# Cross-attention on one core: scores from fp16 pairs, two heads per step, three score banks and two product banks

## The reference

```python
q, k_t, v_t = heads(x @ W_q), heads(text_ehs @ W_k), heads(text_ehs @ W_v)   # 508 text tokens
probs_t = softmax(einsum('bhsd,bhtd->bhst', q, k_t) * Dh ** -0.5)
text_out = einsum('bhst,bhtd->bhsd', probs_t, v_t)
attn_scores = einsum('bhsd,bhnd->bhsn', q, k_ip) * Dh ** -0.5                 # 4 image tokens
qsem = l2norm(einsum('bhst,bte->bhse', probs_t, text_ehs))
sem = einsum('bhse,bne->bhsn', qsem, l2norm(ip_ehs))
probs_ip = softmax(attn_scores + 0.5 * sem) * spatial_mask
out = (text_out + einsum('bhsn,bhnd->bhsd', probs_ip, v_ip)) @ W_out + b_out + x
```

## Time and profile before

| | us |
|---|---|
| median of 3 runs | 1622.18 (1618.69 to 1624.26) |
| profiled execution | 1616.23 |
| span of its trace, first to last instruction | 1614.3 |
| TensorE busy | 1559.7 (97%) |
| VectorE busy | 1306.1 (81%) |
| GpSimd busy | 1257.5 (78%) |
| ACT busy | 1053.4 (65%) |
| mean granted TensorE clock | 0.989 of full speed |

### The profile page before, as it was taken

One profiled execution on the slowest core, in us unless ns is written; L12 is line 12 of the kernel. 1 busy time (PEld: TensorE's weight loads), 2 busy tenths in 40 slices (PEclk: granted clock), 3 DMA queues, 4 the chain that ended last, 5 costly groups with the idle time before them and its releaser, 6 DMA issues.

```text
span 1614.3 us, 39295 instructions
## 1 busy us (share of the span) xinstructions
PE 1559.7 (97%) x13322; PEld 951.1 (59%) x13322; DVE 1306.1 (81%) x3181; ACT 1053.4 (65%) x2289; POOL 1257.5 (78%) x1187
## 2 busy tenths in 40 slices
PE   4999999999999999999999999999999999999996
PEld 2777667556555556555555555555555555555553
DVE  6455563688999978997899789978997899789976
ACT  4455656667776767776777667766776677667761
POOL 4233233789899988997899789988998899889982
PEclk9899999899999999999999999999999999999998
DMA  5455757778789978898889889987898798878963
GB/s 206 132 165 146 202 174 192 151 131 139 134 137 191 154 148 155 164 149 149 153 169 143 148 144 173 147 150 145 171 155 148 147 170 151 148 140 146 160 121 94
DMA packets 656043, 247.89 MB, mean 154 GB/s; under 512 B 619081, under 2 KB 645330, under 8 KB 655858
## 3 DMA queue, kind: packets, MB, share of 16 engines
q1 hardware_dynamic: 654658, 243.75, 78.4%
q10 hardware_dynamic: 1200, 1.80, 0.3%
HBM read 68.51 MB, written 34.55 MB: 64 GB/s over the span
## 4 chain that ended last, share of the span: by engine, by line
PE 78%; DVE 9%; issue 4%; POOL 3%; ACT 3%; DMA 3%; SPq 0%; DVEq 0%; ACTq 0%; POOLq 0%
PE bank L1636 27%; PE bank L1637 17%; PE bank L1689 13%; PE bank L1593 7%; PE bank L1641 3%; PE bank L1603 3%; PE bank L1635 3%; DVE probs L1250 2%; DVE neg_max L1238 2%; DMA late<-wkv 2%; PE bank L1666 2%; PE bank L1750 2%; ACT probs L864 1%; POOL wkv L745 1%; PE bank L1676 1%
## 5 line engine op out<-in xcount | busy, mean ns | idle before, releaser
L1636 PE MATMUL bank<-u_sb,late 127*128 127x508 f16 x2560 | 944.9, 375 | 0.0
L1637 PE MATMUL bank<-u_sb,late 127*128 127x508 f16 (+3 forms) x2560 | 762.1, 298 | 0.0
L1238 DVE TENSOR_REDUCE neg_max<-bank 128x1 f32<-128x508 f32 x640 | 434.7, 679 | 157.4 <-PE bank L1593 156.6
L1635 PE MATMUL bank<-v_ring,late 127*128 127x42 f16 x2560 | 468.2, 183 | 6.9 <-DMA late<-wkv 6.9
L1250 DVE SCALAR_TENSOR_TENSOR probs<-bank,probs 128x508 f32<-128x508 f32 x640 | 431.8, 675 | 5.8 <-PE bank L1637 5.8
L745 POOL TENSOR_TENSOR wkv<-probs,wkv 128x508 f16<-128x508 f32 x320 | 364.8, 1145 | 87.3 <-ACT wkv L876 86.5
L1635 PEld LDWEIGHTS bank<-v_ring,late 127*128 127x128 f16 x2560 | 246.7, 96 | 237.4 <-DMA late<-wkv 8.9
L1636 PEld LDWEIGHTS bank<-u_sb,late 127*128 127x128 f16 x2560 | 247.8, 97 | 185.9 <-issue 1.2
L853 ACT ACTIVATE exp_bias<-neg_max 128x1 f32<-128x1 f32 x512 | 103.8, 203 | 378.5 <-DVE neg_max L1238 376.4
L864 ACT ACTIVATE probs<-bank,exp_bias 128x508 f32<-128x508 f32 x512 | 340.4, 665 | 0.1
L752 POOL TENSOR_TENSOR probs<-probs,wkv 128x508 f32<-128x508 f32 x256 | 290.0, 1143 | 0.0
(11 more groups left out here) (194 smaller groups left out, 1870.6 us busy)
## 6 DMA issues: line engine op xcount, KB each, us to landing
raw<-k_parts SPq DMA_DIRECT2D x192, 79.4 KB, 3.6
raw<-in_ctx_cols SPq DMA_DIRECT2D x8, 1016.0 KB, 7.5
raw<-q_parts SPq DMA_DIRECT2D x32, 240.0 KB, 3.7
...
```

The source lines that it names most:

```text
L1238: nc.vector.tensor_reduce(neg_max[:, v % 4:v % 4 + 1], bank[s_bank(v)][:, 0:T], AX.X, ALU.max, negate=True)\
L1635: nc.tensor.matmul(o, hi_k, v_ring[0:TP, n, h, k, :], start=(k == 0), stop=False)
L1636: nc.tensor.matmul(y, hi_k, u_sb[0:TP, par, GH[k]:GH[k] + T], start=(k == 0), stop=False)
L1637: done = nc.tensor.matmul(y[:, k * TP:T], hi_k, u_sb[0:TP, par, UL[k]:UL[k] + U_COLS[k]], start=False, stop=(k == TT - 1))
```

## The change

- **Scores from fp16 pairs.** Queries and keys are kept as two fp16 parts, unscaled but for a power of two. Their four products are 64 rows. The scale of the scores (`score_unit`) is applied in `shift` and `exp`. All units, plain ones too, get the shift. ACT's casts of the middle part and GpSimd's subtractions in the first phase are gone. Each query part is stored twice.
- **Two heads side by side.** A pair of units, v and v+1, is now heads h and h+10 on the same 128 rows. The score of the first takes rows 0 to 63 of the array, the other one rows 64 to 127. Groups that are loaded together have 4 heads where they had 5.
- **Order.** In every even step TensorE computes both scores of a pair, VectorE both maxima, and ACT shift and exponential of the one and the other, before the rest of either unit.
- **Banks.** Three score banks, two product banks. The products of unit u now need the norm of u-2, and the next pair of scores needs the exponential of the pair's first unit.
- **12 slots of probabilities;** the two more lie in memory that the shorter rings of keys and queries set free.

```diff
-    PAIRS = [(0, 0), (1, 0), (2, 0), (0, 1), (1, 1), (0, 2)]
-    KS = len(PAIRS) * D
+    KS = 4 * D
...
-    PROB_RING, TURN_RING, FLAT_RING, HALF_RING = 10, 7, 8, 4
+    PROB_RING, TURN_RING, FLAT_RING, HALF_RING = 12, 7, 8, 4
...
-    q_parts = nc.dram_tensor("q_parts", [B, 3, D, H, S], bf16).ap()
-    k_parts = nc.dram_tensor("k_parts", [B, 3, D, H, T], bf16).ap()
+    q_parts = nc.dram_tensor("q_parts", [B, 4, D, H, S], fp16).ap()
+    k_parts = nc.dram_tensor("k_parts", [B, 2, D, H, T], fp16).ap()
...
-        parts = late[:, :].bitcast(bf16).rearrange("p (t a s) -> p t a s", t=2 * NC, a=3)
+        parts = late[:, 0:2 * NC * S].bitcast(fp16).rearrange("p (t a s) -> p t a s", t=2 * NC, a=2)
...
-        S_BANKS, PT_BANKS, Y_BANKS, O_BANK = (0, 1), (2,), (3, 4, 5), 6
+        S_BANKS, PT_BANKS, Y_BANKS, O_BANK = (0, 1, 2), (3,), (4, 5), 6
...
+        def place(v):
+
+            pair, rest = divmod(v % OF_BATCH, 2 * ST)
+            return pair + rest % 2 * FAR, rest // 2
...
+        def load_keys(eng, b, i, n):
+
+            for half in range(2):
+                heads = slice(half * FAR + i * GROUP // 2, half * FAR + (i + 1) * GROUP // 2)
+                for copy in range(2):
+                    at = half * KS + copy * 2 * D
+                    eng.dma_start(k_ring[at:at + 2 * D, n], k_parts[b, :, :, heads, :].rearrange("a d h t -> (a d) h t"))\
+                       .then_inc(group_loaded[n], 16)
+
+        def load_queries(eng, b, i, n):
...
-                    dst = (q_parts if t < NC else k_parts)[b].rearrange("a d h s -> (d h) a s")[c0:c0 + cn]
-                    n = S if t < NC else T
-                    sp.dma_start(dst, parts[0:cn, t, :, 0:n]).then_inc(parts_saved, 16)
+                    job = (Q_JOB + K_JOB)[t]
+                    sp.wait_ge(bank_drained[job[0]], use(job, b))
+                    if t < NC:
+                        dst = q_parts[b].rearrange("(a r) d h s -> r (d h) a s", r=2)
+                        for copy in range(2):
+                            sp.dma_start(dst[copy, c0:c0 + cn], parts[0:cn, t, :, 0:S]).then_inc(parts_saved, 16)
+                    else:
+                        dst = k_parts[b].rearrange("a d h s -> (d h) a s")
+                        sp.dma_start(dst[c0:c0 + cn], parts[0:cn, t, :, 0:T]).then_inc(parts_saved, 16)
...
+                if i == 2 and 1 <= g < GROUPS - 1:
+                    next_group(g + 1, load_keys)
+                if i == 5 and 1 <= g < GROUPS - 1:
+                    next_group(g + 1, load_queries)
                 if i == 9 and 1 <= g < GROUPS - 1:
-                    next_group(g + 1)
+                    next_values(g + 1)
...
             def batch(b, first, last):
-
-                for t in range(2 * NC):
-                    cn = CT[t % NC][1]
-                    n = S if t < NC else T
-                    pool.wait_ge(mid_split, 2 * NC * b + t + 1)
-                    nc.gpsimd.tensor_tensor(parts[0:cn, t, 2, 0:n], resid[0:cn, t % R1, 0:n], parts[0:cn, t, 1, 0:n],
-                                            ALU.subtract).then_inc(parts_split, 1)
 
...
             def shift(v):
 
+                b = v // OF_BATCH
                 act.wait_ge(row_max_found, v + 1)
-                nc.scalar.activation(exp_bias[:, v % 4:v % 4 + 1], neg_max[:, v % 4:v % 4 + 1], ACT.Copy, bias=LOG_SCALE)\
-                  .then_inc(bias_ready, 1)
+                nc.scalar.activation(exp_bias[:, v % 4:v % 4 + 1], neg_max[:, v % 4:v % 4 + 1], ACT.Identity, bias=log_col[:, 0:1],
+                                     scale=score_unit[:, b:b + 1]).then_inc(bias_ready, 1)
 
             def exp(v):
 
-                if is_turned(v):
-                    act.wait_ge(bias_ready, nth(v) + 1)
-                else:
-                    act.wait_ge(row_max_found, v + 1)
+                b = v // OF_BATCH
+                act.wait_ge(bias_ready, v + 1)
                 need(act, norms_done, v + 1 - PROB_RING)
-                bias = exp_bias if is_turned(v) else neg_max
-                nc.scalar.activation(probs[:, v % PROB_RING, :], bank[s_bank(v)][:, 0:T], ACT.Exp,
-                                     bias=bias[:, v % 4:v % 4 + 1]).then_inc(probs_ready, 1)
+                if PROB_SLOTS <= v < PROB_RING:
+                    act.wait_ge(in_lo_split, 2 * B)
+                nc.scalar.activation(prob(v), bank[s_bank(v)][:, 0:T], ACT.Exp, bias=exp_bias[:, v % 4:v % 4 + 1],
+                                     scale=score_unit[:, b:b + 1]).then_inc(probs_ready, 1)
 
             def flat_hi(v):
...
 
                 b, j = batch_of(v)
-                if v < TT and is_turned(v):
+                if v < TT:
                     shift(v)
+                    exp(v)
+                elif v < UNITS and v % 2 == 0:
+                    shift(v)
+                    exp(v)
+                    shift(v + 1)
+                    exp(v + 1)
                 if v >= HI_AT and not is_turned(v - HI_AT):
                     hi(v - HI_AT)
-                if v < UNITS:
-                    exp(v)
-                if TT <= v + 1 < UNITS and is_turned(v + 1):
-                    shift(v + 1)
...
-
-
...
                 for t in range(2 * NC):
                     j, c0, cn = (Q_JOB + K_JOB)[t], *CT[t % NC]
                     act.wait_ge(bank_filled[j[0]], use(j, b))
                     if t < NC:
                         nc.scalar.activation(q_full[0:cn, t, :], bank[j[0]][0:cn, 0:S], ACT.Identity,
                                              scale=scale[0:cn, par, Q_COL:Q_COL + 1]).then_inc(q_full_ready, 1)
-                        nc.scalar.activation(parts[0:cn, t, 0, 0:S], bank[j[0]][0:cn, 0:S], ACT.Identity,
-                                             scale=scale[0:cn, par, Q_COL:Q_COL + 1]).then_inc(hi_split, 1)
+                        nc.scalar.activation(parts[0:cn, t, 0, 0:S], bank[j[0]][0:cn, 0:S], ACT.Copy, scale=HEAD_DOWN).then_inc(hi_split, 1)
                     else:
-                        nc.scalar.activation(parts[0:cn, t, 0, 0:T], bank[j[0]][0:cn, 0:T], ACT.Identity,
-                                             scale=scale[0:cn, par, K_COL:K_COL + 1]).then_inc(hi_split, 1)
-                    if t > 0:
-                        middle(t - 1)
+                        nc.scalar.activation(parts[0:cn, t, 0, 0:T], bank[j[0]][0:cn, 0:T], ACT.Copy, scale=HEAD_DOWN).then_inc(hi_split, 1)
...
@@ -1440,8 +1463,11 @@
             def unit(v):
 
                 b, j = batch_of(v)
-                if v < UNITS:
+                if v < TT:
                     row_maximum(v)
+                elif v < UNITS and v % 2 == 0:
+                    row_maximum(v)
+                    row_maximum(v + 1)
                 u = v - NORM_AT
...
-                    n, col = (S, Q_COL) if t < NC else (T, K_COL)
+                    n = S if t < NC else T
                     dve.wait_ge(hi_split, 2 * NC * b + t + 1)
-                    dve.wait_ge(parts_split, 2 * NC * b + t + 1)
-                    nc.vector.scalar_tensor_tensor(resid[0:cn, t % R1, 0:n], bank[j[0]][0:cn, 0:n], scale[0:cn, par, col:col + 1],
+                    nc.vector.scalar_tensor_tensor(parts[0:cn, t, 1, 0:n], bank[j[0]][0:cn, 0:n], HEAD_DOWN,
                                                    parts[0:cn, t, 0, 0:n], ALU.mult, ALU.subtract)\
...
                 for t in range(NC):
                     residual(t)
                 if not last:
...
             def scores(v):
 
-                g, h, st = v // OF_GROUP, v // ST % GROUP, v % ST
-                n = g % 2
+                g, st, half, pr = v // OF_GROUP, place(v)[1], v % 2, v // (2 * ST) % 2
+                n, rows = g % 2, slice(half * KS, (half + 1) * KS)
                 if v % OF_GROUP == 0:
-                    pe.wait_ge(group_loaded[n], 16 * 9 * (g // 2 + 1))
+                    pe.wait_ge(group_loaded[n], 16 * 6 * (g // 2 + 1))
                 if v < len(S_BANKS):
                     pe.wait_ge(bank_drained[s_bank(v)], end_of_phase1(s_bank(v)))
-                need(pe, probs_ready, v + 1 - len(S_BANKS))
-                nc.tensor.matmul(bank[s_bank(v)][:, 0:T], q_ring[:, n, h, st * P:(st + 1) * P], k_ring[:, n, h, :],
+                need(pe, probs_ready, v - v % 2 + 2 - len(S_BANKS))
+                nc.tensor.matmul(bank[s_bank(v)][:, 0:T], q_ring[rows, n, pr, st * P:(st + 1) * P], k_ring[rows, n, pr, :],
...
-                if v + LEAD < UNITS:
+                y, o = bank[y_bank(v)][:, 0:T], bank[O_BANK + st % 2][:, half * VCOLS:(half + 1) * VCOLS]
+
+                if v % 2 == 0 and v + LEAD < UNITS:
                     scores(v + LEAD)
+                    scores(v + LEAD + 1)
...
                 need(pe, norms_done, v + 1 - len(Y_BANKS))
-                if st % 2 == 0:
+                if half == 0:
```

127 lines of the change are left out of this document (67 added, 60 removed).

## The result

The changed kernel takes 1755.3 us (median of four runs, 1751.58 to 1755.9). The kernel before, on the same chip, takes 1623.22 us (1618.69 to 1624.87). The ratio is 1.0809, with an interval of 1.0787 to 1.0831: the change makes the kernel 132 us slower. Forecast were 1753 us. The profiled execution took 1751.58 us around a span of 1749.9, which is 135.6 longer than the span of the earlier trace rows.

A forecast was written before the change was run, and what follows sets the result against it. TensorE bound the old kernel; a closed TensorE-VectorE loop would bound the new one. Profiled 1616.2 + 135 (8 x 16.9) - 2 - 2 = 1747, median 6 above: 1753 us, range 1700 to 1790 (0.78).

The forecast's parts named there:

- The circle: Closed loop per unit pair between TensorE and VectorE (scores, two maxima, norm, odd unit's products): 4.14 us a pair.
- release to product: From the norm's end on VectorE to TensorE's first waiting product: 0.14 us taken, 0.04 as bound from below.
- way into half rows: On TensorE, going from full-row products into half-row scores costs 0.10 us inside the loop; bounds 0 and 0.30.
- rival with 0.04 and no switch: The loop holds, but the norm's release takes 0.04 us and switching nothing: 3.94 a pair, 1689 us; chance 0.06.
- dearer rival: Loop holds; switches cost 0.30, or scores run singly with VectorE late at batch closings: 1785 to 1820 us; chance 0.08.
- The second pass: On VectorE, the norm of units 9, 19, ... has another pass before signalling: 0.67 us more per ten units.
- The transposes: On TensorE ahead of odd units' products, 0.44 us per four: taken as no cost, 18 us kept for the range.
- The batch: An attention batch of eighty units takes 178.8 us against 161.95, +16.9, with 1 us left for small stalls.
- The first phase: Projections, bound by TensorE: no gain in their loop; 2 us saved at the turn into attention.
- B: No closed loop; TensorE sets the pace and switches eat the score overlap: 1619 us, no change; chance 0.03.
- A: No closed loop; TensorE sets the pace, scores run side by side without switch cost: 1555 us, faster; chance 0.05.
- Cost 0: ACT's added shifts and new order cost nothing: exponential ends about s + 2.1 us, next scores need it at s + 4.1.

The follow-up runs named there:

- 1625.09: Changed kernel with two score banks and three product banks in place of three and two, its order kept (also called three-bank kernel): 1625.09 us.
- full rows: The three-bank kernel (1625.09) with each score matmul on all 128 rows, so two scores cannot stand side by side: 1624.0 us.
- 1631.26: Changed kernel with the norm ahead of both maxima on VectorE, and ACT's cast of the upper half one step earlier: 1631.26 us.
- the old forms: Changed kernel with shift and exponential as in the kernel before (constant addend, no scale from memory): 1756.83 us.
- the norm first: Changed kernel with the norm of v-9 placed ahead of both maxima on VectorE: 1677.12 us.
- the order alone: Changed kernel with VectorE again alternating one maximum and one norm; paired scores, three score and two product banks stay: 1749.12 us.
- the kernel that goes unit by unit: Kernel with two score and three product banks; half-row scores, maxima, shifts, exponentials and their wait go singly instead of in pairs: 1735.42 us.
- the kernel with both repairs: Changed kernel with two score and three product banks, norm ahead of both maxima, and the upper half's cast one step earlier: 1692.59 us.

## Why the prediction was right, point by point

**The circle.** Every step of the sum has its counterpart in the pair shown above:

| step | forecast | measured |
|---|---|---|
| scores to first maximum | 0.41 | 984.83 to 985.25: 0.42 |
| two maxima | 1.20 | 985.25 to 986.45: 1.20 |
| norm, to the end of its read | 0.68 | 986.45 to 987.13: 0.68 |
| release to product | 0.14 | 987.13 to 987.28: 0.15 |
| products | 1.61 | 987.28 to 988.88: 1.60 |
| way into half rows | 0.10 | 984.74 to 984.83: 0.09 |
| sum | 4.14 | 4.14; pairs elsewhere 4.16 (980.67 to 984.83) |

The way in is that of the scores at 984.83: the last products of the pair before start at 984.64 and fill 0.10. The release, for which the prediction had no row of its own, only ACT's 0.14 and 0.04 as a bound from below, is 0.15; all 132 waits of over 0.1 us that a norm or a second pass ends between 560 and 1540 us show 0.14 to 0.16. The rival with 0.04 and no switch falls with it. The 0.30 of the dearer rival was a guess that no row had shown; the ways of 0.09 and 0.10 answer it.

**The second pass** was put at 0.67 once in ten units. Four units take 10.00 us without it and 10.66 with it (809.99 to 820.65).

**The transposes** were taken to be hidden, with 18 us held back for the other case. In three pairs of five there are none ahead of the odd products: 192 pairs in all. The waits are 188, 63 of them behind the second pass (66.8 / 63 = 1.06 each) and 125 plain ones (49.0 / 125 = 0.39 each), against 0.36 + 0.67 = 1.03 and 0.36. The two pairs with transposes wait for nothing: they fill the gap. Their size was wrong, though. Four transposes were put at 0.44; in the kernel after they take 0.52 behind products and 0.54 to 0.55 behind half-row scores:

```profile
982.61 0.69 PE L1630 MATMUL bank<-ident,raw 128*127 128x128 f32 x4
983.13 0.19 PE L1663 MATMUL bank<-v_ring,late 127*128 127x42 f16 x1
```

So TensorE's own work in such a pair is 0.32 + 0.53 + 1.61 + 1.60 + 0.09 = 4.15, as long as the circle. It cost nothing because it fell into the gap, which is luck; where the circle is open it counts: 16 sets a batch at 0.09, 1.4 us, some 11 us in all (an estimate from these rows). Why transposes are dearer in those two places no run shows.

**The batch** was put at 178.8, 1.0 of it for small stalls, and takes 179.0. Forecast for eight were 135 us; 8 x 17.05 are 136.4.

**The first phase.** No gain in its loop, as worked out. The chain's first group behind the projections starts 3.65 us earlier (276.84 instead of 280.49), all of it from an earlier start of the projection loop (46.34 instead of 49.97); 2 were forecast. The 2 were expected from the turn into the attention, and that is not where the gain came. The ramp into the attention costs about 3 us that the sum did not have: from the start to the first output product lie 141 units, at 0.213 more each (17.05 / 80) 30.0 us; less 3.65 that is 26.4, and 29.7 are measured.

**The sum.** The profiled execution was put at 1747 and took 1751.58, 4.6 more: 1.4 in the batches, 3.3 in the ramp, 1.6 at the end (the last 19 units cost 0.4 us less than their share, where 2 were forecast), less 1.6 in the first phase. The median was then put 6 us above the profiled execution and lies 3.7 above it. That 1753 misses 1755.3 by only 2.3 us is therefore in part luck; the +16.9 us a batch, measured as 17.05, are not.

**The rivals without the circle.** They gave TensorE's own pace as 1555 (half rows free to enter) or 1619 (switches eat the overlap). Three runs open the circle: 1625.09, 1624.0 (full rows) and 1631.26. So B's reasoning is the right one for an open loop, and A's is not: of the score pair 0.21 us are saved and two ways of 0.10 are paid. B came out some us too low since it did not have the dearer transposes: four units with one set of them take 9.49 us in the three-bank kernel, 0.07 more than before. The second score does run beside the first: from the pair to the next product the changed kernel takes 0.32 us, with one score by itself 0.31.

```profile
908.56 0.39 PE L1620 MATMUL bank<-raw 64*128 64x508 f16 x2
908.88 0.19 PE L1663 MATMUL bank<-v_ring,late 127*128 127x42 f16 x1
```

By the Trainium skill, TensorE: Matmul & The Clock Gate, Part 3, matmuls in different row groups run together, about 4 ns apart; these 0.01 us, the smallest step that the trace shows, agree. By the Trainium skill, TensorEngine Tiling (Array Packing), Key Properties, a change of the mode drains the engine. That section gives no size, and the measured 0.09 and 0.10 us are just enough to make the pairing worth nothing beside full-row work.

**What the prediction had too cheap: ACT.** The groups of the kernel after, count and busy time and mean ns of one:

```profile
L886 ACT ACTIVATE exp_bias<-neg_max,log_col,score_unit 128x1 f32<-128x1 f32 x640 | 243.5, 381 | 287.9 <-DVE neg_max L1260 287.9
L896 ACT ACTIVATE probs<-bank,exp_bias,score_unit 128x508 f32<-128x508 f32 x534 | 413.7, 775 | 17.8
```

A shift takes 0.38 us and an exponential 0.78, where 0.20 and 0.67 were used. The estimate that the exponential ends about s + 2.1 was too low: the new operands of both were left out, and in the pair above it ends at 987.16, which is s + 2.3. "Cost 0" held all the same, which the run with the old forms shows (1756.83, no gain), because the next scores need it at s + 4.1. It held only under the cover that the circle gave. With the norm first, the same ACT work cost 33 us.

By the Trainium skill, ScalarE: Activation LUTs, What ACT_TABLE_LOAD costs, each 128x1 pointer operand adds some 93 ns to an activation. Two more on the shift and one more on the exponential are what these kernels have. The two forms in otherwise the same kernel, the changed one, take 381 against 198 ns and 775 against 685 ns: +0.18 and +0.09 us, which agrees.

**Where my expectations behind the prediction failed.** The forecasts for the order alone (1647 against 1749.12 measured) and for the norm first (1610 against 1677.12) took the two maxima for the whole cause and the upper half's cast for free. The prediction named both halves of the cause, the second maximum and the bank; the runs show that giving back the bank is enough by itself, and giving back the old order is not.

**The ramp with three product banks.** The first output product comes 10 us later than before (591.32 against 581.27) though the batches are 0.4 us shorter. Two stretches have this time. From 285 to 320 us TensorE does 171 matmuls in place of 227: its scores wait 9.3 us for exponentials there, against 4.0 before, and the mean granted clock is 0.76 against 0.85. From 360 to 480 us it does 1048 in place of 1089, with 5.6 us of waits for exponentials against 3.3. Together that is 97 matmuls, some 10.6 us at the 1481 in 162 us of the earlier trace rows (an estimate). This points at the paired order with two score banks, which makes scores wait longer at places where the kernel before waits too; in the kernel that goes unit by unit the waits from 285 to 320 us are 5.8.

**Open.** How the 126 us of the alternating order split between the cast and the closing work; why transposes are dearer behind products and behind half rows; and which of its two edits makes the kernel with both repairs slow. None of the versions beats the kernel before: 1624.0, 1625.09 and 1631.26 are the nearest.
